# Second and last product of the third layer's FFN as three float32r products on halves

## The reference, cut to what matters

```
# L1: routing with scores, attention with a decay, and 8 experts
h = gelu(einsum('nd,efd->enf', xf, w1));  y_e = einsum('enf,edf->end', h, w2)
y = einsum('ne,end->nd', scores_sel, y_e)

# L2: attention of 8 heads (softmax over 512 keys), and a gated FFN of width 512
h = silu(xn @ w1.T * s1) * (xn @ w2.T * s2)      # 128 -> 512
h = gelu(h @ h1.T * sh1)                         # 512 -> 512, "h1"
h = gelu(h @ h2.T * sh2)                         # 512 -> 512, "h2"
y = h @ w3.T * s3                                # 512 -> 128, "y"
```

## Time and profile before

| | |
|---|---|
| three executions | 1970.83, 1971.64, 1975.49 us |
| profiled execution: its time | 1971.33 us |
| profiled execution: first to last instruction | 1969.5 us |
| PE busy | 1790.3 us (91%) |
| DVE busy | 980.9 us (50%) |
| ACT busy | 842.7 us (43%) |
| POOL busy | 237.9 us (12%) |
| mean granted TensorE clock | 0.951 |

### The profile page before, as it was taken

One profiled execution on the slowest core, in us unless ns is written; L12 is line 12 of the kernel. 1 busy time (PEld: TensorE's weight loads), 2 busy tenths in 40 slices (PEclk: granted clock), 3 DMA queues, 4 the chain that ended last, 5 costly groups with the idle time before them and its releaser, 6 DMA issues. The chain is left out here.

```text
span 1969.5 us, 22671 instructions
## 1 busy us (share of the span) xinstructions
PE 1790.3 (91%) x8518; PEld 1004.5 (51%) x8518; DVE 980.9 (50%) x1612; ACT 842.7 (43%) x1021; POOL 237.9 (12%) x205
## 2 busy tenths in 40 slices
PE   6589999998887999999999999999999979999996
PEld 4222222224443436676758585858676644444442
DVE  3454454444655444444444344434444446677765
ACT  4467777774323333333334333333433343443442
POOL 1000000000542001010101010000101022233222
PEclk8799999998767999999999999999999989999998
DMA  1222222222004630000000000000000010000001
GB/s 70 46 44 44 44 44 44 44 44 112 1 1 117 142 85 1 1 1 1 1 1 1 1 1 1 1 1 1 1 1 0 1 51 1 0 0 0 0 0 43
DMA packets 19116, 48.90 MB, mean 25 GB/s; under 512 B 784, under 2 KB 1552, under 8 KB 18000
## 3 DMA queue, kind: packets, MB, share of 16 engines
q1 hardware_dynamic: 19024, 47.63, 10.3%
HBM read 45.14 MB, written 2.36 MB: 24 GB/s over the span
## 5 line engine op out<-in xcount | busy, mean ns | idle before, releaser
L494 ACT ACTIVATE probs<-ps_ring 128x1024 f32<-128x1024 f32 x256 | 246.1, 1023 | 123.8 <-PE ps_ring L708 121.1
L1716 PEld LDWEIGHTS ps_o<-v,probs 128*128 128x128 f32 x2048 | 236.5, 192 | 34.7 <-issue 31.5
L1716 PE MATMUL ps_o<-v,probs 128*128 128x129 f32 x2048 | 250.8, 279 | 1.7 <-ACT probs L1459 1.2
L1459 ACT ACTIVATE probs<-ps_ring 128x1024 f32<-128x1024 f32 x128 | 127.0, 1024 | 242.1 <-PE ps_ring L1697 242.0
L1529 DVE TENSOR_REDUCE negmax<-ps_o 128x2 f32<-128x1024 f32 x64 | 78.5, 1226 | 167.0 <-PE ps_o L1672 167.0
L722 PE MATMUL ps_o<-probs,v 128*32 128x512 f32 x1024 | 139.2, 617 | 13.1 <-DVE o_sb L545 13.1
L1451 ACT ACTIVATE probs<-ps_ring,pack 128x512 f32<-128x512 f32 x64 | 40.5, 685 | 180.9 <-PE ps_ring L1645 105.5
L1645 PE MATMUL ps_ring<-probs,pack 128*128 128x512 f32 x256 | 117.2, 602 | 0.0
L1542 DVE RECIPROCAL rden<-ps_o 128x2 f32<-128x2 f32 x128 | 21.5, 168 | 178.8 <-PE ps_o L1716 178.8
L1909 POOL TENSOR_TENSOR rs<-r,state 128x512 f32<-128x512 f32 x64 | 81.7, 1276 | 205.6 <-DVE state L2001 202.0
L708 PEld LDWEIGHTS ps_ring<-q_stack,k_stack 32*128 32x128 f32 x512 | 31.7, 187 | 124.6 <-issue 99.7
(11 more groups left out here) (359 smaller groups left out, 3253.1 us busy)
## 6 DMA issues: line engine op xcount, KB each, us to landing
cwb<-combine_by_expert SPq DMA_DIRECT2D x8, 2048.0 KB
score<-score_by_expert SPq DMA_DIRECT2D x7, 2048.0 KB, 13.9
pack<-pack_dram SPq DMA_DIRECT2D x1, 2560.0 KB, 13.7
pack<-pack_dram SPq DMA_DIRECT2D x1, 2443.0 KB, 9.3
x<-x_in SPq DMA_DIRECT2D x2, 1024.0 KB, 6.0
out<-x SPq DMA_DIRECT2D x1, 2048.0 KB, 6.3
score<-score_by_expert SPq DMA_DIRECT2D x1, 1536.0 KB, 13.4
pack<-pack_dram SPq DMA_DIRECT2D x1, 1451.0 KB, 8.0
```

What stands on the lines that cost most here:

```text
L494: nc.scalar.activation(probs[n % 3][:, 2 * half:2 * half + 2, :], ps, ACT.Exp, scale=float(HD0) ** -0.5).then_inc(read, 1)
L1459: nc.scalar.activation(probs[:, n % 2, m, :, :], ps, ACT.Exp).then_inc(read, 1)
L1716: last = nc.tensor.matmul(ps_o[:, i, k * (D + 1):(k + 1) * (D + 1)], probs[:, (b * PAIRS + p) % 2, m, j, queries], v[:, m, h, :], start=(m ...
```

## The change

Three parts.

1. The weights of h2 and w3 move from pack "third_whole" into pack "third", which grows from 5120 to 7680 columns, and with it the copy of line 1173 and the subtraction of line 1166. The two packs together stay as large.
2. `hide2` and `down` use `split_products`. ACT's gelus write the raw value to `th` or `raw` (SBUF, buffers of the gates that are free by then); DVE rounds it into a high half (`split_hidden`, 8 copies a batch), and POOL subtracts to a low one (8 a batch). TensorE waits for each low half. A PSUM slot of h1 or h2 is now released by DVE after its two copies, not by ACT after its two gelus. DVE's copies are placed between its maxima.
3. To find room in SBUF: halves of hidden lie in `xh`, `xl`, the gates' buffers and two new tiles; `xc`, `sq`, `xb`, `th` and `raw` of `layer2_mix` lie in `xn`; in `layer1_route_and_attend` `xc` lies in `attended1` and `tie` in the second half of that, so that POOL's clearing is cut in two: the first half after the layer norm, the second ahead of batch 4, after `ranked`.

```diff
@@ packed @@
         "h1_2": tiles_of_rows(f["L2_ffn_h1_w"].T),
+        "h2_2": tiles_of_rows(f["L2_ffn_h2_w"].T),
+        "w3_2": tiles_of_rows(f["L2_ffn_w3_w"].T),
     }
     third_whole = {
         "ones_row2": k["ones_row"],
-        "h2_2": tiles_of_rows(f["L2_ffn_h2_w"].T),
-        "w3_2": tiles_of_rows(f["L2_ffn_w3_w"].T),
@@ layer1_route_and_attend @@
-        xc = sb("n1_xc", [P, NTOK])
+        xc = sh["attended1"][:, :, :].rearrange("p b t -> p (b t)")
-        tie = sb("n1_tie", [P, NT, E1, E1])
+        tie = xc[:, NTOK // 2:].rearrange("p (t e f) -> p t e f", e=E1, f=E1)
...
-            nc.gpsimd.memset(o[DS:P, :, :], 0.0)
+            pool.wait_ge(normed, B)
+            nc.gpsimd.memset(o[DS:P, 0:B // 2, :], 0.0)
...
             for b in range(B + 1):
+                if b == B // 2:
+                    pool.wait_ge(ranked, 1)
+                    pool.drain()
+                    nc.gpsimd.memset(o[DS:P, B // 2:, :], 0.0)
+                    pool.drain()
@@ layer2_mix: buffers @@
-        flat = probs[:, :, :, :, :].rearrange("p a m j t -> p (a m j) t")
-        hidden = {"h1": flat[:, 8:12, :], "h2": flat[:, 12:16, :]}
+        hid_high, hid_low = sb("hid_high2", [P, T]), sb("hid_low2", [P, T])
+        gate = [(gate_high[:, t, :], gate_low[:, t, :]) for t in range(FT)]
+        hidden = {"h1": [(xh, xl), (hid_high, hid_low), gate[0], gate[1]],
+                  "h2": [gate[2], gate[3], (xh, xl), (hid_high, hid_low)]}
...
+        def hid_raw(t):
+            return (th if t < 2 else raw)[:, t % 2, :]
@@ gpsimd, per batch after the gates @@
+                for n, name in enumerate(("h1", "h2")):
+                    for t in range(FT):
+                        pool.wait_ge(hid_high_ready, (2 * b + n) * FT + t + 1)
+                        nc.gpsimd.tensor_tensor(single(hidden[name][t][1][:, :]), hid_raw(t), hidden[name][t][0][:, :], ALU.subtract
+                                                ).then_inc(hid_low_ready, 1)
@@ scalar: tanh @@
+                if b and t < 2:
+                    act.wait_ge(hid_low_ready, (2 * b - 1) * FT + t + 1)
@@ scalar: gelu @@
-                        last = nc.scalar.activation(hidden[n][:, t, :], ps[:, j, :], ACT.Gelu, scale=w[scale][:, t:t + 1])
-                    last.then_inc(read, 1)
+                        act.wait_ge(hid_low_ready if n == "h2" else gate_low_ready, (2 * b * FT if n == "h2" else b * FT) + t + 1)
+                        nc.scalar.activation(hid_raw(t), ps[:, j, :], ACT.Gelu, scale=w[scale][:, t:t + 1]).then_inc(hid_ready, 1)
@@ vector @@
+            def split_hidden(b, name, i):
+                n = (2 * b + ("h1", "h2").index(name)) * FT
+                ps, read = filled(dve, (name, b, i))
+                for t in range(2 * i, 2 * i + 2):
+                    dve.wait_ge(hid_ready, n + t + 1)
+                    nc.vector.tensor_copy(single(hidden[name][t][0][:, :]), hid_raw(t)).then_inc(hid_high_ready, 1)
+                dve.drain()
+                dve.sem_inc(read, 1)
...
-                for m in range(NBLK):
-                    maximum(b, 0, m)
+                maximum(b, 0, 0)
+                maximum(b, 0, 1)
+                split_hidden(b, "h1", 0)
+                maximum(b, 0, 2)
+                maximum(b, 0, 3)
+                split_hidden(b, "h1", 1)
                 take_rows(b, 0)
-                for m in range(NBLK):
-                    maximum(b, 1, m)
+                maximum(b, 1, 0)
+                split_hidden(b, "h2", 0)
+                maximum(b, 1, 1)
+                maximum(b, 1, 2)
+                split_hidden(b, "h2", 1)
+                maximum(b, 1, 3)
@@ tensor: hide2 @@
-                    if i == 0 and kt % 2 == 0:
-                        was_read(pe, ("h1", b, kt // 2))
+                    if i == 0:
+                        pe.wait_ge(hid_low_ready, 2 * b * FT + kt + 1)
...
-                        last = nc.tensor.matmul(ps[:, j, :], w["h2_2"][:, kt * T + t * P:kt * T + (t + 1) * P],
-                                                hidden["h1"][:, kt, :], start=(kt == 0), stop=(kt == FT - 1))
+                        last = split_products(nc, ps[:, j, :], weight("h2_2", kt * T + t * P),
+                                              tuple(part[:, :] for part in hidden["h1"][kt]), kt == 0, kt == FT - 1)
@@ tensor: down @@
-                    if kt % 2 == 0:
-                        was_read(pe, ("h2", b, kt // 2))
-                    last = nc.tensor.matmul(ps[:, 0, :], w["w3_2"][:, kt * P:(kt + 1) * P], hidden["h2"][:, kt, :],
-                                            start=(kt == 0), stop=(kt == FT - 1))
+                    pe.wait_ge(hid_low_ready, (2 * b + 1) * FT + kt + 1)
+                    last = split_products(nc, ps[:, 0, :], weight("w3_2", kt * P),
+                                          tuple(part[:, :] for part in hidden["h2"][kt]), kt == 0, kt == FT - 1)
```

More of the change, by code:

```diff
@@ L1073, in _ @@
             nc.vector.reduce_sum(rank[:, :, :], first[:, :, :, :], AX_X)
-            nc.vector.tensor_tensor(tie[:, :, :, :], first[:, :, :, :],
+            nc.vector.tensor_tensor(tie, first[:, :, :, :],
                                     pr[:, :, :].unsqueeze(2).broadcast_to([P, NT, E1, E1]), ALU.mult)
             dve.drain()
-            nc.vector.reduce_sum(mass[:, :, :], tie[:, :, :, :], AX_X)
+            nc.vector.reduce_sum(mass[:, :, :], tie, AX_X)
             dve.drain()
@@ L1325, in layer2_mix @@
         sem = lambda name: ctx.enter_context(nc.semaphore(name))
-        xc, sq, xb = sb("xc2", [P, T]), sb("sq2", [P, T]), sb("xb2", [P, T])
+        xc, sq, xb = (sh["xn"][:, at(i)] for i in range(3))
         xh, xl = sb("xh2", [P, T]), sb("xl2", [P, T])
@@ L1332, in layer2_mix @@
         probs = sb("probs2", [P, 2, NBLK, 2, T])
-        flat = probs[:, :, :, :, :].rearrange("p a m j t -> p (a m j) t")
-        hidden = {"h1": flat[:, 8:12, :], "h2": flat[:, 12:16, :]}
         gate_high, gate_low = sb("gate_high2", [P, FT, T]), sb("gate_low2", [P, FT, T])
-        th, raw = sb("tanh2", [P, 2, T]), sb("raw2", [P, 2, T])
+        th, raw = (sh["xn"][:, at(i, 2 * T)].rearrange("p (t n) -> p t n", n=T) for i in (2, 3))
+        hid_high, hid_low = sb("hid_high2", [P, T]), sb("hid_low2", [P, T])
+        gate = [(gate_high[:, t, :], gate_low[:, t, :]) for t in range(FT)]
+        hidden = {"h1": [(xh, xl), (hid_high, hid_low), gate[0], gate[1]],
+                  "h2": [gate[2], gate[3], (xh, xl), (hid_high, hid_low)]}
         half_s1, s12 = sb("half_s1", [P, FT]), sb("s12", [P, FT])
@@ L1355, in layer2_mix @@
         gate_high_ready, gate_low_ready = sem("gate_high_ready2"), sem("gate_low_ready2")
+        hid_ready, hid_high_ready, hid_low_ready = sem("hid_ready2"), sem("hid_high_ready2"), sem("hid_low_ready2")
         sh_loaded = [sem("sh_loaded2_0"), sem("sh_loaded2_1")]
@@ L1508, in take_low @@
                                         ALU.subtract).then_inc(read, 1)
+            def split_hidden(b, name, i):
[6 more added lines that the diff above has]
+                dve.sem_inc(read, 1)
             def take_gate(b, t):
                 n = b * FT + t
+                if b and t < 2:
+                    dve.wait_ge(hid_low_ready, (2 * b - 1) * FT + t + 3)
                 dve.wait_ge(tanh_ready, n + 1)
```

## The result

The changed kernel took 1959.45 us (median of 7, 1955.12 to 1966.82) where the kernel before took 1973.09 (median of 7 on the same chip, 1970.83 to 1977.28): ratio 0.993, interval 0.9909 to 0.9951, 13.6 us less (interval 9.7 to 18). The forecast was 1962.3, 9.3 us less than the 1971.64 it was set against. The profiled execution took 1955.12 us, the fastest of the seven; its span is 1953.2 us against 1969.5.

The account below looks back on a forecast made before the run. TensorE was taken to bound the kernel, busy 98.39 of 100 us in the third layer; 1971.33 - 23.5 + 6.7 + 7.6 gave 1962.1, forecast as 1962.3 us, with 1954.5 to 1969.5 as the range for 8 in 10.

Parts of the forecast that it names:

- TensorE's work: Third layer, h2 and y: split products save 2.41 and 0.63 less 0.1 at the turn, 2.94 us a batch, 23.5 in all.
- The second layer: Start of layer1_experts: wider packs lengthen ACT's copy by 2.1 and POOL's subtraction by 5.5 us, unhidden: +7.6, ends 5.5 and 9.
- rival A: Stops in h2 and y, or layer1_experts' price, not paid: 1955.4 us without the stops, 1954.5 without the price; chance 0.14.
- New waits: Third layer: TensorE stops 0.35 after the turn and 0.35 before y, plus 0.07 per restart: 0.84 a batch, 6.7 us.
- if POOL starts after the second copy: First h2 half: POOL waits for DVE's second copy, low halves at T0 + 3.83 and 5.13; otherwise 2.4 us faster.
- the hand-overs: Third layer, between engines: POOL starts 0.08 after a copy's end, TensorE goes on 0.15 after a low half is written.
- The rest: Second layer's split memset falls into POOL's idle time, DMA bytes stay the same, moved buffers cost nothing; 1.8 if cover were gone.
- Sum: Whole kernel: 1971.33 - 23.5 + 6.7 + 7.6 = 1962.1 us, 1962.4 against the median; forecast 1962.3, 0.47% less.
- Rival B: Third layer: gelus or copies 0.3 to 0.7 later at both stops, 1.4 to 2.2 a batch; about 1969 us; chance 0.20.
- C: h2 and y: POOL's subtractions become the bound at 2.15 instead of 1.30 each, 30 us, 1985 in all; chance 0.03.
- D: h2 and y: stops drop TensorE's clock to 1.2 GHz, costing 12 to 25 us, 1975 to 1987 in all; chance 0.03.

Follow-up runs that it names:

- e8: Changed kernel with two terms for all ternary third-layer weights, copies ahead of the maximum, narrow subtraction in pieces, high-half products first in h2 and y; 1876.07 us.
- e1: Changed kernel with h2 and y as plain products again, without the copies and subtractions of hidden, wide packs and moved buffers kept; 1980.67 us, 1.0039 to before.
- e2: Changed kernel with POOL's subtraction of 7680 columns cut into 15 instructions of 512; 1942.14 us, ratio 0.9862.
- e7: Changed kernel with one more DVE copy of 1024 columns, read by nobody, between the two copies of each second half; 1984.75 us in a single execution.
- e5: Kernel before with only the moved buffers of layer1_route_and_attend and POOL's clearing in two halves; 1969.91 us, ratio 0.9996.

## Why the prediction was right, point by point

*TensorE's work*: 23.5 us forecast. The trace gives 15.30 - 13.03 = 2.27 in h2 and 4.26 - 3.62 = 0.64 in y. The 2.27 still has the stop of 0.28 after the turn in it; without it 3.19 a batch are saved, 25.5 us. The runs of 2.98 and 1.60 are there. The 2.0 us too few are the turn and the run ahead of it: the turn takes 0.03 by e8 instead of the 0.21 allowed, the run 2.90 instead of 2.98.

*The second layer*: 7.6 forecast, 7.4 in the trace and 7.4 in the trace of e1, which does this part alone (7.7 by its times). ACT's copy 6.61 (4.47 + 2.14), POOL 16.35 (16.7 expected), TensorE's stop 13.94 (about 15 expected). e2 shows the mechanism. Right, and rival A's half of it falls.

*New waits*: 6.7 forecast, two stops a batch of 0.42 each. This is the mis-sized term. Both stops are there, where and by whom forecast, but they are 0.28 and 0.23 long: 4.1 us. The steps that failed are "if POOL starts after the second copy" and the hand-overs. Forecast: POOL starts at T0 + 2.53, its low half is written at T0 + 3.83, TensorE goes on at T0 + 3.98. Measured: start at T0 + 2.17 beside the second copy, written at T0 + 3.58 (1.41 instead of 1.30), TensorE on at T0 + 3.64 (0.06 behind POOL instead of 0.15). TensorE would have been there at T0 + 3.35, not 3.6, which gives back part of what the earlier POOL saves. In y the second copy ends at T + 2.43 and y starts 0.10 later, not 0.27. The rule of the Trainium skill (page "SBUF — State Buffer", section "Who interferes with whom") that who starts first has the ports for the whole instruction agrees with e7 in both directions, where what is held comes in about 0.15 before the end of the other. I took it to cost 0.35 a batch here; it costs 0.12 (1.39 against 1.27), since the rest of the second copy was short when POOL started.

*The rest*: nothing forecast; e5 measures nothing (0.9996). A stop of 0.34 in batch 1 before the first head, by the exponentials, was not foreseen; it is in one of eight batches; another of 1.2 us in that place was there before.

*Sum*: by the terms -25.5 + 7.4 + 4.1 = -14.0, where the forecast had -9.2: 2.6 of the difference are the stops, 2.0 TensorE's own work, 0.2 the second layer. From turn to turn a batch is 105.38 before and 102.77 now (mean of seven), 2.61 less, where the terms give 3.19 - 0.51 = 2.68. The table has -20.0 + 7.4 = -12.6 for the two blocks; the difference to -14.0 is the lower clock at the layer's end (1.1) and the stop in batch 1 (0.3). The times say -13.6 with an interval of -9.7 to -18, so the forecast's amount lies just outside it, and that the median came within 3 us of 1962.3 says less than it seems: the seven executions reach from 1955.12 to 1966.82. Rival A came true only in part of its stops (2.6 of 6.7 us). Rival B did not occur, C not either (1.27 to 1.41 a subtraction). Nor did D here: the granted clock is 1.00 in the stretch with the stops. But its mechanism exists, at stops of 1.83, in four of e7's eight batches.

## What to carry to other kernels

When an operation is made faster by operands that need preparing, price the preparation where it runs: here a third of the gain was lost in another layer, because one long POOL instruction keeps a DVE instruction with two SBUF inputs waiting to its end. Cut such instructions into pieces; that alone gave as much again as the change did. Look for stops in the intervals between starts, and in the rows of the weight loads, not in the busy share alone: a stop of 0.28 in every batch stood in neither TensorE's busy time nor its list of waits. And ask of a split product which of its halves is zero: weights of -1, 0 and 1 need two terms.

## What the runs showed of the hardware that was not expected

Cut into pieces, POOL's work takes 23.34 us instead of 16.35 while DVE works beside it, and the kernel is 15.6 us faster. After a stop of 1.83 us TensorE's granted clock fell to the lower level in four of eight batches of e7, and stayed at 1.00 after the other four. The time at which the same program reaches a place in its second layer differs by 8.4 us between two executions (600.36 and 608.80), with TensorE's mean granted clock at 0.951 and 0.947, while the stretches behind agree to 0.1 us. A difference of 3 us between two profiles must therefore be taken apart by stretch before it is explained.
